# Two rows of softmax maxima leave through two DMA queues, and TensorE waits for them in front of the products that read them

## The reference

```
n = groupnorm(x)                       # x: 8 x 768 x 32 x 32, 32 groups
q, k, v = Wq n, Wk n, Wv n             # 1x1 convolutions, 12 heads of 64
attn = softmax(q^T k / 8)              # 1024 x 1024 per head, 96 heads
out  = x + Wp (v attn^T)
```

## Time and profile before

| | |
|---|---|
| median of 3 runs | 3404.21 us (3401.08 to 3405.39) |
| the profiled execution's own time | 3401.64 us |
| its span | 3399.8 us |
| granted TensorE clock, mean | 0.994 |
| start of the first `scores_by_key` (pair 0) | 1256.74 us |
| busy share of the span | PE 98%, POOL 54%, DVE 52%, ACT 32% |

### The profile page before, as it was taken

How to read it: one execution, slowest core, us unless ns; L and a number is a source line. 1 busy time by engine, 2 the same in 40 slices (tenths; PEclk the granted TensorE clock), 3 DMA queues, 4 the chain that set the end, 5 groups by cost and what they waited for, 6 DMA issues and landing times.

```text
span 3399.8 us, 51561 instructions
## 1 busy us (share of the span) xinstructions
PE 3321.5 (98%) x18272; PEld 2252.7 (66%) x18272; DVE 1784.2 (52%) x2417; ACT 1089.1 (32%) x1944; POOL 1833.6 (54%) x789
## 2 busy tenths in 40 slices
PE   7999999999999979999999999999999999999999
PEld 6888888888888854445555555555555555555557
DVE  5333323233233147776666666666666666666652
ACT  3111111111111114444444444444444444444441
POOL 2000000000000029998888888888888888888883
PEclk9999999999999979999999999999999999999999
DMA  6232433423243342334434434344344344343434
GB/s 234 103 137 105 146 130 123 147 99 137 101 145 109 112 152 81 118 122 144 152 118 151 149 132 162 119 162 156 124 155 150 121 143 154 125 162 125 156 106 167
DMA packets 221700, 461.90 MB, mean 136 GB/s; under 512 B 22961, under 2 KB 73009, under 8 KB 220209
## 3 DMA queue, kind: packets, MB, share of 16 engines
q1 hardware_dynamic: 221488, 459.16, 38.7%
HBM read 259.06 MB, written 199.62 MB: 135 GB/s over the span
## 4 chain that ended last, share of the span: by engine, by line
PE 56%; DMA 3%; issue 2%; DVE 1%; SPq 1%; POOL 1%; ACT 0%; ACTq 0%; POOLq 0%; DVEq 0%
PE psum L746 20%; PE psum L759 19%; PE psum L769 10%; PE psum L731 7%; PE psum L828 1%; DMA recip_rows<-compact 1%; DMA top<-turned 1%; DVE half_max L902 1%; POOL sums L702 0%; ACT p_all L862 0%; SPq L573 0%; SPq L582 0%; DMA k<-k_parts 0%; DVE flipped L912 0%; DVE compact L941 0%
## 5 line engine op out<-in xcount | busy, mean ns | idle before, releaser
L702 POOL TENSOR_TENSOR sums<-sums,p_all 128x1024 f32<-128x1024 f32 x576 | 1352.8, 2392 | 0.0
L902 DVE TENSOR_REDUCE half_max<-psum 128x2 f32<-128x1024 f32 x768 | 939.1, 1224 | 514.7 <-PE psum L731 496.7
L862 ACT ACTIVATE p_all<-psum 128x512 f32<-128x512 f32 x1536 | 792.9, 601 | 925.0 <-PE psum L746 920.8
L759 PE MATMUL psum<-p_all,v 128*64 128x512 f32 x3072 | 743.4, 605 | 0.0
L746 PE MATMUL psum<-q,k 64*128 64x512 f32 x4608 | 672.6, 397 | 20.6 <-DMA top<-turned 17.8
L710 POOL TENSOR_TENSOR wp<-sums,wp 128x1536 fp32r<-128x1536 f32 x1 | 3.4, 3449 | 1176.9 <-ACT wp L888 1176.9
L746 PEld LDWEIGHTS psum<-q,k 64*128 64x128 f32 x4608 | 427.1, 185 | 136.7 <-ACT p_all L862 34.3
L240 PE MATMUL psum<-xn_hi,w_hi 128*128 128x512 f32 x1128 | 439.6, 390 | 0.6 <-DVE stage L380 0.6
L240 PE MATMUL psum<-xn_hi,w_lo 128*128 128x512 f32 x1128 | 439.0, 389 | 0.0
L240 PE MATMUL psum<-xn_lo,w_hi 128*128 128x512 f32 x1128 | 439.0, 389 | 0.0
L290 ACT CAST stage<-psum 128x512 fp32r<-128x512 f32 x192 | 112.7, 588 | 961.6 <-PE psum L240 951.5
(11 more groups left out here) (78 smaller groups left out, 2569.2 us busy)
## 6 DMA issues: line engine op xcount, KB each, us to landing
q_parts<-stage SPq DMA_DIRECT2D x192, 256.0 KB, 2.2
k_parts<-stage SPq DMA_DIRECT2D x192, 256.0 KB, 2.3
q<-q_parts SPq DMA_DIRECT2D x48, 1024.0 KB, 5.0
k<-k_parts SPq DMA_DIRECT2D x48, 1024.0 KB, 7.4
a<-o_parts SPq DMA_DIRECT2D x84, 512.0 KB, 7.6
v_rows<-stage SPq DMA_DIRECT2D x128, 192.0 KB, 2.1
v<-v_rows SPq DMA_DIRECT2D x48, 512.0 KB, 4.7
recip_all<-recip_rows SPq DMA_DIRECT2D x96, 256.0 KB, 3.9
```

What stands on the lines that cost most here:

```text
L702: pool.tensor_tensor(sums[:, m % 2, i, :], first, p_all[:, i, n, :], ALU.add).then_inc(added, 1)
L759: mm = pe.matmul(heads[part, h, :], v[:, e, t, part], p_all[:, i, (m * MT + t) % EXPS, cols], start=(t == 0), stop=(t == MT - 1))
L862: act.activation(p_all[:, i, (m * MT + t) % EXPS, h * BANK:(h + 1) * BANK], psum[:, SCORE_BANKS[2 * h + i], :], ACT.Exp, scale=SCALE).then ...
L902: dve.tensor_reduce(half_max[:, :, t, h], of, AX.X, ALU.max, negate=True).then_inc(max_done, 1)
```

## The change

Three things are done. Head B's DMA of each pair is issued by ScalarE, in a new function `second_maxima`, with the same wait on `neg_done`; SyncE keeps head A's. ScalarE calls it for pair p + 1 behind the last `exponent` of pair p and in front of `take_heads`, and for pair 0 at the start of the phase, in front of the five copies of wp. And TensorE's wait for both DMAs of a pair is put in front of the first product with c = 3, behind the six products with c < 3.

```
-                for i in range(2):
-                    sp.dma_start(f32(top[i * DH:i * DH + 1, m % SLOTS, :]).rearrange("a (t n) -> a t n", t=MT),
-                                 f32(turned[i * MT:(i + 1) * MT, m % 2, :])).then_inc(top_in, 16)
+                sp.dma_start(f32(top[0:1, m % SLOTS, :]).rearrange("a (t n) -> a t n", t=MT),
+                             f32(turned[0:MT, m % 2, :])).then_inc(top_in, 16)
...
-                if t == 0 and h == 0:
-                    pe.wait_ge(top_in, 32 * (p + 1))
...
                 for c in range(4):
+                    if t == 0 and h == 0 and c == 3:
+                        pe.wait_ge(top_in, 32 * (p + 1))
...
+            def second_maxima(p, m):
+                act.wait_ge(neg_done, p + 1)
+                act.dma_start(f32(top[DH:DH + 1, m % SLOTS, :]).rearrange("a (t n) -> a t n", t=MT),
+                              f32(turned[MT:2 * MT, m % 2, :])).then_inc(top_in, 16)
...
+                    if t == MT - 1 and not (known(p) and p == NP - 1):
+                        second_maxima(p + 1, m + 1)
                     if t == HIGH_AT and at_least(p, 2):
                         high_out(p - 2, m - 2)
 
+            act.wait_ge(set_done, SETS)
+            second_maxima(0, 0)
             act.wait_ge(wp_in, 16 * len(wp_raw))
```

## The result

The changed kernel takes 3419.32 us (median of 6 runs, 3417.51 to 3421.25) against 3403.99 us (median of 6 runs, 3401.01 to 3405.39): a ratio of 1.0046, 95% interval 1.0036 to 1.0056. It is 15.3 us slower; forecast was 3403.4, range 3396 to 3411.

The account below looks back on a forecast made before the run. TensorE was taken as the bound, GpSimd in pairs 3 to 6. 3401.64 + 9.7 (start) - 9.2 (shorter waits) gave 3402.1 us on the profiled execution, 3404.7 on the median; forecast between them 3403.4, range 3396 to 3411.

Parts of the forecast that it names:

- What bounds the kernel: Whole kernel: TensorE is busy 98% of the span; its 16 waits for `top`, 17.8 us, are the waits' own ceiling.
- The cost at the start, 9.7 us: Second phase's start: ScalarE's DMA delays its wp copies; 7.8 us later plus 1.9 us of slow clock, range 7.0 to 10.3.
- What a wait gets shorter by, 1.38 us: Each wait for `top`: 0.70 us from products run meanwhile plus 0.68 us from issuing DMAs side by side; at least 0.70.
- Pairs 1 to 6, 1.7 us, and pairs 7 and 8, 1.65 + 1.4: Gains: pairs 1 and 2 1.7 us, pairs 3 to 6 none as GpSimd sets the pace, pair 7 1.65, pair 8 1.4.
- Pairs 9 to 47, 4.5 us: Pairs 9 to 47, where TensorE is the bound: all seven waits for `top` go, gaining 4.5 us, by the lower value 2.4.
- What costs nothing, and its cover: At turns of pairs: ScalarE's DMA issue is covered by 0.6 then 4.6 us; a wait already met costs TensorE nothing.
- The second: Rival, middle of a block: the wait exposes a weight load, 48 x 0.184 = 8.8 us, 3410.9 (3413.5 on the median); chance 0.10.
- The first: Rival: GpSimd doesn't hold pairs 3 to 6 and clock returns, 3392.7, or the start costs only part, 3392.4; together 0.12.
- The third: Rival, waits for `top`: head A's row stays last, only 0.70 us saved per wait, pair 7 gains nothing, +5.3 us; chance 0.15.

Follow-up runs that it names:

- The mended start: Changed kernel, but for pair 0 SyncE sends both rows, so ScalarE begins the phase with its copies of wp: 3408.21 us, ratio 1.0015.
- The queue alone: Changed kernel with TensorE's wait back at the head of the block, head B's DMA still on ScalarE: 3409.44 us, ratio 1.0020.
- the moved wait alone, with 11 more: Kernel before with only TensorE's wait moved, both DMAs on SyncE, and 11 more TensorE instructions ahead of its loop: 3391.90 us, ratio 0.9967.
- both mended: Changed kernel with SyncE sending both rows for pair 0 and 11 more TensorE instructions ahead of its loop: 3390.63 us, ratio 0.9964.
- the kernel with 11 more: Changed kernel with 11 more TensorE instructions, made by 21 already met waits, ahead of its loop of six pairs: 3402.38 us, ratio 0.9999.
- the wait alone: Kernel before with only TensorE's wait moved in front of the products that read `top`, both DMAs on SyncE: 3408.12 us, ratio 1.0018.
- before with 245 more: Kernel before with 245 more TensorE instructions, already met waits, ahead of and between the first 16 coarse units: 3427.73 us, ratio 1.0073.

## Why the prediction was wrong

It was wrong by a term that it didn't have. The kernel with the change and 11 idle instructions has every edge that I priced and lacks only that term: it takes 3402.38 us, where the sum was 3402.1 on the profiled execution and 3404.7 on the median. That it comes so near is in part luck: the start costs 10.8 us in it where the sum had 9.7, and the stretches behind gain 3.9 + 5.4 + 0.9 = 10.2 where it had 9.2.

- **What bounds the kernel.** Right: TensorE, with 17.8 us to get.
- **The cost at the start, 9.7 us.** Measured 10.73. ScalarE took 1.24 us to issue its first DMA where I took 0.8, and the third `scores_by_key` is 8.2 us later, not 7.8; the other 2.5 us, where I had 1.9, I put down to the clock, 0.50 over 4.1 us and 0.69 over the 3.1 us behind it. The mended start gives the whole back. The upper end was 10.3, so it lies just outside.
- **What a wait gets shorter by, 1.38 us.** The two parts don't simply add. The queue alone took 4.6 us off 17.8, the moved wait alone, with 11 more, 11.7, both together 11.3 (both mended). The 0.70 of the products does it alone: in the wait alone with 11 more the waits of pairs 2 to 7 are 0.42 to 0.56 us and behind pair 8 one of 0.50 is left; with the second queue too (both mended) they are 0.25 to 0.75 and 0.23. At pair 8 the wait remains 2.6 to 2.7 us with or without the queue.
- **Pairs 1 to 6, 1.7 us, and pairs 7 and 8, 1.65 + 1.4.** Measured 2.28 (pairs 1 to 7) and 1.73 (7 to 12, of which 0.9 from pair 7 to 8 and 0.8 from 8 to 9): 4.0 where 4.75 was the sum, the early pairs a little better and pairs 7 and 8 little more than half. GpSimd did hold pairs 3 to 6: it is busy in 181.00 of 181.00 us there, as in the earlier trace rows,

```profile
1352.00:1533.00 181.00, 174.16 (x1092) 88.20 (x1090) 131.46 (x158) 90.01 (x166) 181.00 (x78) 1.00 0.32 116
```

  but I expected ScalarE to wait for it. It waits 2.4 us, once, as it did before. VectorE's transposes of the sums wait for it 3.6 us (1.7 before), and TensorE for VectorE's maxima 2.3 us (0.2 before).
- **Pairs 9 to 47, 4.5 us.** 5.4 in the loop and 0.9 behind it in the kernel with 11 more: 6.3. That is 1.8 us more than the waits themselves, and no run shows where it comes from. TensorE's waits for `top` from 1600 us on are one, 0.23 us, in the changed kernel, against the earlier trace rows.
- **"What costs nothing, and its cover".** This is the step that failed. It says that the moved wait costs TensorE nothing because a wait already met doesn't. True of its time to run; but an instruction also has a place, and 11 fewer of them moved the loop's entry. That cost 18.4 us, more than any term that the sum had. The order that I quoted shows that no matmul has moved; it does not show instructions that only wait. The four stops of 1.1 to 1.6 us at the jumps back, which the list of before has under "issue", were a sign that jumps cost TensorE something, and I rested on none of them.
- **The rivals.** The second came nearest by its number (3411 to 3413.5) and its site, a moved wait that costs more than nothing, and is wrong: a wait in the middle of a block costs nothing, since the kernel with 11 more instructions has 48 of them. In the changed kernel too the first products with `top` of pair 18 start 0.70 us behind those with `k` (2021.05 and 2020.35 us), as before (2009.03 and 2008.33). The first is excluded by the busy GpSimd and by 48.61 us. A part of it did happen: behind the wait of pair 7 the granted clock was 1.00 in 1528.2 to 1531.7 us, where the earlier trace rows has 0.59, and still only 0.9 us came of it from pair 7 to 8. Its price has a slip: by the row, 1.5 us of the wait at pair 7 remain and not 0.5, which gives 3393.7 instead of 3392.7. The third was right in that the second queue adds nothing to the moved wait, and at pair 8 the wait did lose just the 0.70 (3.29 to 2.6 to 2.7 us). Its price was wrong, since the moved wait alone gave 11 us. The chance of slower, 0.14, was too small for a sum of two terms of nearly 10 us that cancel.

## What to carry to other kernels

Where a loop is so long that its instructions are fetched again in each turn (here one of 3322, and not the first phase's of 1502), count the instructions ahead of the entry, waits too: an edit that adds or removes a few of them can cost or give more than what it is for. If the time moves without a reason in the work, look at the first products behind each jump back, and put some idle instructions ahead of the loop before judging the edit. And a wait placed on an engine's queue holds everything behind it, so the first turn of a pipeline, where other work still stands in that queue, has to be priced on its own.

## What the runs showed of the hardware

- A jump back costs TensorE 1.1 to 1.75 us in every kernel here. A second stop of 1.3 to 2.2 us comes when the block of 256 instructions ends 11 instructions behind the entry, and none when it ends 40 behind it, or 256.
- The block behind the one that is jumped into is fetched only once TensorE runs again: its fetch starts 0.6 to 1.5 us behind the first instruction after the jump, in all ten kernels and at all four jumps.
- A loop of 1502 instructions was turned five times more without a fetch of TensorE's instructions; one of 3322 was fetched anew in each turn: from the first jump to the second 14 blocks before and 15 in the changed kernel.
- The stop's larger part is what follows. The four second stops of the changed kernel are 7.6 us, and the loop's loss is 18.4. The eight products, broken in two and six, take 1.07 + 1.93 us instead of 1.94, which is 4.2 us for four jumps. The slow clock costs the six products and the group 6.8 us: after two idle stretches of 1.5 and 2.1 us with four products between them, it was 0.50 for 3.7 us. It does not always fall: in one kernel (the start mended) the six products behind a stop of 1.42 us took 1.93 us, in the next jump, behind 2.19 us, 3.67. It fell at 11 of the 16 second stops in the four kernels that have them, behind 1.54 to 2.19 us; the five without a fall are 1.28 to 1.88 us long.
- Three of these four kernels scatter more. The standard deviation of their times is 2.6 us (the wait alone), 2.3 (the start mended) and 3.5 (before with 245 more), against 0.5 to 1.9 in the kernels without second stops; the changed kernel's own is 1.3, from 6 executions.
- Instructions that only wait, and for what has long been reached, are not free in number: 245 of them ahead of and between the first 16 coarse units delayed the first issue into `top` by 7.5 us, 216 by 5.3 us, though TensorE had been waiting for VectorE there. 11 can't be seen.
